# Reordering TensorE's round in a one-core image tower: second norm's turn, base products, gated turn, and who joins the turned fold

## The reference

```
h = patches(x) @ W                                  # 64 x 196 tokens, 768 -> 256
n = layernorm(h)                                    # first norm
x_proj = n @ in_w + in_b
mod    = gelu(n @ mod_w1 + mod_b1) @ mod_w2 + mod_b2        # 256 -> 1024 -> 256
y      = irfft(rfft(x_proj * mod) * rfft(kernel))   # over the 196 tokens of an image
h = h + y @ out_w + out_b
n = layernorm(h)                                    # second norm
base   = n @ base_W.T + base_b
shared = (n @ shared_A.T) @ shared_B.T
w      = softmax(n @ router_W.T + router_b), the two largest of six kept and scaled to sum 1
h = h + base + shared + sum over experts e of w_e * (n @ routed_A_e.T) @ routed_B_e.T
```

## Time and profile before

| what | value |
|---|---|
| time, median of 3 runs | 1248.58 us (1248.07 to 1249.25) |
| the profiled execution: its time, its span | 1247.64 us, 1245.8 us |
| granted TensorE clock, mean | 0.999 of full speed |
| busy: PE, PEld | 1223.9 us (98%), 1175.7 us (94%) |
| busy: DVE, ACT, POOL | 888.8 us (71%), 643.2 us (52%), 406.9 us (33%) |
| chain that ended last | PE 80%, DVE 9%, ACT 7%, issue 2%, DMA 1% |
| DMA, mean over the span | 59 GB/s |

### The profile page before, as it was taken

The page is one execution under the profiler, slowest core; times in us unless marked ns, Lnnn a source line. Parts: engine busy times, 40 slices in busy tenths (PEclk is TensorE's granted clock), DMA queues, the critical chain, the costliest instruction groups (busy, mean ns, idle before and its releaser), DMA issues.

```text
span 1245.8 us, 20849 instructions
## 1 busy us (share of the span) xinstructions
PE 1223.9 (98%) x7914; PEld 1175.7 (94%) x7914; DVE 888.8 (71%) x2591; ACT 643.2 (52%) x1197; POOL 406.9 (33%) x459
## 2 busy tenths in 40 slices
PE   9999999999999999999999999999999999999998
PEld 8899999999999999999999999999999999999996
DVE  6477766677766777766777666777667777667777
ACT  6645555545555445555455555455554445454432
POOL 3523244332244232343232443323442323433220
PEclk9999999999999999999999999999999999999999
DMA  7310222221322111222202222212221112211001
GB/s 244 94 49 20 68 69 68 56 34 47 69 69 68 56 28 55 69 68 56 59 23 68 69 68 56 33 49 68 68 69 55 26 57 68 68 56 33 14 13 34
DMA packets 85089, 72.97 MB, mean 59 GB/s; under 512 B 64775, under 2 KB 78958, under 8 KB 81150
## 3 DMA queue, kind: packets, MB, share of 16 engines
q1 hardware_dynamic: 84990, 71.66, 20.4%
HBM read 43.07 MB, written 12.85 MB: 45 GB/s over the span
## 4 chain that ended last, share of the span: by engine, by line
PE 80%; DVE 9%; ACT 7%; issue 2%; DMA 1%; SPq 1%; POOL 0%; ACTq 0%; DVEq 0%
PE rotating L1457 16%; PE rotating L1458 15%; PE rotating L1459 15%; PE rows_ps L1457 8%; PE rows_ps L1458 6%; PE rows_ps L1459 6%; PE turn L1744 5%; PE turn L1507 2%; PE rows_ps L1517 2%; ACT gelu_h L661 2%; DVE y_l L1161 1%; ACT y_h L698 1%; ACT gelu L656 1%; DVE gelu_l L1106 1%; DVE gated_l L1186 1%
## 5 line engine op out<-in xcount | busy, mean ns | idle before, releaser
L529 POOL TENSOR_TENSOR folded<-modulated 128x196 f32<-128x196 f32 x63 | 38.1, 605 | 565.0 <-DVE modulated L1118 565.0
L656 ACT ACTIVATE gelu<-rotating,consts 128x392 f32<-128x392 f32 x256 | 145.4, 582 | 109.2 <-PE rotating L1459 108.9
L514 POOL TENSOR_TENSOR gelu_l<-gelu,gelu_h 128x784 fp32r<-128x784 f32 x62 | 128.7, 2075 | 213.1 <-DVE norm L1101 172.0
L509 POOL TENSOR_TENSOR patches_l<-patches,patches_h 128x384 fp32r<-128x384 f32 (+1 forms) x186 | 182.1, 1008 | 2.8 <-ACT patches_h L608 2.8
L1457 PE MATMUL rotating<-x_h,w_h 128*128 128x392 f32 x512 | 177.2, 346 | 1.6 <-ACT gelu L656 1.6
L1457 PE MATMUL rotating<-gelu_h,w_h 128*128 128x392 f32 x512 | 177.4, 346 | 0.0
L1458 PE MATMUL rotating<-x_l,w_h 128*128 128x392 f32 x512 | 174.6, 341 | 0.0
L1459 PE MATMUL rotating<-x_h,w_l 128*128 128x392 f32 x512 | 174.6, 341 | 0.0
L1458 PE MATMUL rotating<-gelu_l,w_h 128*128 128x392 f32 x512 | 174.2, 340 | 0.0
L1459 PE MATMUL rotating<-gelu_h,w_l 128*128 128x392 f32 x512 | 174.0, 340 | 0.0
L1457 PE MATMUL rows_ps<-tokw_h,patches_h 128*128 128x256 f32 x570 | 162.9, 286 | 1.5 <-DVE patches_l L871 1.5
(11 more groups left out here) (300 smaller groups left out, 2997.7 us busy)
## 6 DMA issues: line engine op xcount, KB each, us to landing
patches<-dram_x_rest SPq DMA_DIRECT2D x30, 1152.0 KB, 5.2
out<-h_sb SPq DMA_DIRECT2D x30, 384.0 KB, 2.5
prod<-spec_y SPq DMA_TRANSPOSE x60, 3.2
patches<-dram_x_first SPq DMA_DIRECT2D x2, 384.0 KB, 5.7
h_sb<-dram_x_second SPq DMA_DIRECT2D x1, 768.0 KB, 7.6
patches<-dram_x_fourth SPq DMA_DIRECT2D x1, 768.0 KB, 9.6
h_sb<-dram_first SPq DMA_DIRECT2D x2, 320.0 KB, 3.5
gelu<-dram_w SPq DMA_DIRECT2D x1, 512.0 KB, 8.1
```

The lines of the kernel that those rows point to most:

```text
L509: pool.tensor_tensor(patches_l[:, k, 0:n], patches[:, k, 0:n], patches_h[:, k, 0:n].bitcast(F32), ALU.subtract).then_inc(pool_patches_lo, 1)
L514: pool.tensor_tensor(gelu_l[:, 2 * j:2 * j + 2, :], gelu[:, 2 * j:2 * j + 2, :], gelu_h[:, 2 * j:2 * j + 2, :].bitcast(F32), ALU.subtract)\
L529: pool.tensor_tensor(folded[:, m, 0, :, 1:NF], fwd, back, ALU.add)
L656: act.activation(gelu[:, k, :], bank(g + 1, UP[k])[:, 0:GT], ACT.Gelu, bias=b1_bias[:, k:k + 1]).then_inc(act_gelu, 1)
```

## The change

Four things move, none is computed otherwise.

1. **Second norm's turn ahead of the intake's.** `turn_x2` stood behind all of `mlp_down` 1; it now stands behind three of its eight parts, two parts ahead of `turn_x1`. Since it writes over `rows_ps`, which ScalarE's first norm reads, it also waits for `act_norm1`. ScalarE and VectorE take `x2_hi`, `x2_lo` ahead of `x1_hi`, `x1_lo`.
2. **Base products ahead of the projection.** `base_route(tail)` and with it VectorE's gate come before `project(mid)`.
3. **Gated turn behind four up blocks.** `turn_gated` moves from behind `mlp_up` 5 to behind `mlp_up` 3, `routed` from behind 6 to behind 5, `dft` from behind 7 to behind `routed`, `inverse_dft` from behind `embed` 1 to behind `embed` 0. ScalarE's `gated_hi` and `fold_hi` go ahead of its fifth gelu, VectorE's products of spectra ahead of its `gelu_lo` of the third pair.
4. **VectorE joins both halves.** `sine_whole` goes away; `join_fold` is two copies on VectorE, one behind the other, ahead of `gated_lo`.

The diff, cut to its core:

```diff
-IN, UP, TURN_GATED, OUT, DOWN = (0, 1), (2, 3, 4, 5, 6, 7, 9, 10), 8, 11, (12, 13)
+IN, UP, TURN_GATED, OUT, DOWN = (0, 1), (2, 3, 4, 5, 7, 8, 9, 10), 6, 11, (12, 13)
-TURN_AT = 5
+TURN_X2_AT, TURN_X1_AT = 3, 5
...
             def fold_hi(g):
-                    act.wait_ge(act_whole, g + 1)
-                    act.wait_ge(dve_whole, g + 1)
+                    act.wait_ge(dve_whole, 2 * g + 2)
...
                 gelu_tile(mid, 0)
-                if in_range(back):
-                    sine_whole(back)
                 gelu_tile(mid, 1)
+                gelu_hi(mid, 0)
                 gelu_tile(mid, 2)
-                gelu_hi(mid, 0)
                 gelu_tile(mid, 3)
-                gelu_tile(mid, 4)
                 if in_range(tail):
                     gated_hi(tail, bank(i, TURN_GATED))
                 if in_range(back):
                     fold_hi(back)
+                gelu_tile(mid, 4)
+                gelu_hi(mid, 1)
                 gelu_tile(mid, 5)
-                gelu_hi(mid, 1)
...
-            def cosine_whole(g):
+            def join_fold(g):
                 dve.wait_ge(fold_turned, 32 * (g + 1))
-                dve.tensor_copy(whole_halves[0:NF, 0], turned_halves[0:NF, :, 0, :]).then_inc(dve_whole, 1)
+                for x in range(2):
+                    dve.tensor_copy(whole_halves[0:NF, x], turned_halves[0:NF, :, x, :]).then_inc(dve_whole, 1)
...
                 else:
+                    if in_range(tail):
+                        base_route(tail, rows_ps, x2_h, x2_l)
                     project(mid)
-                if in_range(tail):
-                    base_route(tail, rows_ps, x2_h, x2_l)
...
                 mlp_up(mid, 3)
                 pe.wait_ge(act_gelu, HC * mid + 2)
+                if in_range(tail):
+                    turn_gated(tail, bank(i, TURN_GATED))
+                pe.wait_ge(act_gelu, HC * mid + 3)
                 mlp_up(mid, 4)
-                pe.wait_ge(act_gelu, HC * mid + 3)
+                pe.wait_ge(act_gelu, HC * mid + 4)
                 mlp_up(mid, 5)
-                pe.wait_ge(act_gelu, HC * mid + 4)
-                if in_range(tail):
-                    turn_gated(tail, bank(i, TURN_GATED))
-                pe.wait_ge(act_gelu, HC * mid + 5)
-                mlp_up(mid, 6)
                 if in_range(tail):
                     routed(tail, rows_ps)
-                pe.wait_ge(act_gelu, HC * mid + 6)
-                mlp_up(mid, 7)
                 if in_range(back):
                     dft(back)
+                mlp_up(mid, 6)
+                pe.wait_ge(act_gelu, HC * mid + 5)
+                mlp_up(mid, 7)
...
                 embed(i + 1, 0)
-                embed(i + 1, 1)
                 if in_range(back):
                     inverse_dft(back)
+                embed(i + 1, 1)
...
+                if in_range(back):
+                    mlp_down(mid, 1, range(TURN_X2_AT))
+                    pe.wait_ge(act_norm1, i + 2)
+                    turn_x2(back, rows_ps, norm2)
+                    mlp_down(mid, 1, range(TURN_X2_AT, turn_at))
...
                 turn_x1(i + 1)
                 mlp_down(mid, 1, range(turn_at, HC))
-                if in_range(back):
-                    turn_x2(back, rows_ps, norm2)
 
             last = GROUPS - 1
+            base_route(last - 2, rows_ps, x2_h, x2_l)
             project(last)
             turn_fold(last - 1)
-            base_route(last - 2, rows_ps, x2_h, x2_l)
```

More of the change, by code:

```diff
@@ L836, in _ @@
             gelu_tile(last, 3)
+            gated_hi(last - 2, bank(GROUPS, TURN_GATED))
             gelu_tile(last, 4)
@@ L1359, in _ @@
                 if in_range(back):
-                    cosine_whole(back)
+                    join_fold(back)
                 if in_range(tail):
@@ L1366, in _ @@
                     finish(tail, rows_ps)
-                for j in range(0 if i == 1 else 2, 3):
-                    gelu_lo(mid, j)
                 if in_range(back):
@@ L1372, in _ @@
                     spectrum_of_y(back)
+                for j in range(0 if i == 1 else 2, 3):
+                    gelu_lo(mid, j)
                 gelu_lo(mid, 3)
@@ L1392, in _ @@
                 modulate(mid, 0)
+                if in_range(back):
+                    x2_lo(back, rows_ps, x2_h, x2_l)
                 if i == 1:
@@ L1792, in _ @@
                 else:
+                    if in_range(tail):
+                        base_route(tail, rows_ps, x2_h, x2_l)
                     project(mid)
-                if in_range(back):
-                    if back == 0:
-                        pe.wait_ge(weight_lo, len(LATER))
-                if in_range(tail):
-                    base_route(tail, rows_ps, x2_h, x2_l)
                 if in_range(mid - 1):
@@ L1811, in _ @@
                 mlp_up(mid, 4)
[L1812 removed]
+                pe.wait_ge(act_gelu, HC * mid + 4)
                 mlp_up(mid, 5)
[L1814 to L1818 removed]
                 if in_range(tail):
                     routed(tail, rows_ps)
[L1821 to L1822 removed]
+                if back == 0:
+                    pe.wait_ge(weight_lo, len(LATER))
                 if in_range(back):
                     dft(back)
+                mlp_up(mid, 6)
+                pe.wait_ge(act_gelu, HC * mid + 5)
+                mlp_up(mid, 7)
                 if in_range(tail):
@@ L1840, in _ @@
                     embed(i + 1, 2)
+                pe.wait_ge(act_gelu, HC * mid + 6)
                 if in_range(back):
@@ L1846, in _ @@
                 pe.wait_ge(act_gelu, HC * mid + 8)
-                turn_at = 2 if i == 1 else TURN_AT
-                mlp_down(mid, 1, range(turn_at))
-                if i >= 2:
+                turn_at = 2 if i == 1 else TURN_X1_AT
+                if in_range(back):
+                    mlp_down(mid, 1, range(TURN_X2_AT))
+                    pe.wait_ge(act_norm1, i + 2)
+                    turn_x2(back, rows_ps, norm2)
+                    mlp_down(mid, 1, range(TURN_X2_AT, turn_at))
                     pe.wait_ge(dve_y, DH * back + DH)
                     pe.wait_ge(dve_h, i - 1)
+                else:
+                    mlp_down(mid, 1, range(turn_at))
                 turn_x1(i + 1)
                 mlp_down(mid, 1, range(turn_at, HC))
-                if in_range(back):
-                    turn_x2(back, rows_ps, norm2)
             last = GROUPS - 1
+            base_route(last - 2, rows_ps, x2_h, x2_l)
             project(last)
             turn_fold(last - 1)
-            base_route(last - 2, rows_ps, x2_h, x2_l)
             pe.wait_ge(dve_mod, DH * last)
@@ L1870, in _ @@
             pe.wait_ge(act_gelu, HC * last + 2)
+            turn_gated(last - 2, bank(GROUPS, TURN_GATED))
+            pe.wait_ge(act_gelu, HC * last + 3)
             mlp_up(last, 4)
-            pe.wait_ge(act_gelu, HC * last + 3)
+            pe.wait_ge(act_gelu, HC * last + 4)
             mlp_up(last, 5)
-            pe.wait_ge(act_gelu, HC * last + 4)
-            turn_gated(last - 2, bank(GROUPS, TURN_GATED))
+            routed(last - 2, rows_ps)
+            mlp_up(last, 6)
             pe.wait_ge(act_gelu, HC * last + 5)
-            mlp_up(last, 6)
-            pe.wait_ge(act_gelu, HC * last + 6)
-            routed(last - 2, rows_ps)
             mlp_up(last, 7)
```

9 lines of the change are left out of this document (1 added, 8 removed).

## The result

The changed kernel takes 1343.63 us (median of 4 runs, 1342.46 to 1344.88); the kernel before, on the same chip, 1248.32 (1247.79 to 1249.25). The ratio is 1.0763, 95% interval 1.0744 to 1.0781: 7.6% slower. The forecast of 1235.5 has the wrong sign, and the time lies above its range. The profiled execution took 1343.86 us, its span is 1340.7.

A forecast was written before the change was run, and what follows sets the result against it. TensorE's list of products was the bound, so only its standing time could be won: -31.9 + 7 + 3 + 5 + 2.6 + 1.3 = -13.0 from 1247.64, 1234.6, as a median 1235.5 us; range 1220 to 1268.

The forecast's parts named there:

- The 5.80: Time from the gate's start to the joining copy on VectorE, putting that copy at 8.97 us after the first base product.
- the stall before `routed`: TensorE's wait for the low part of the gated rows; claimed to go wholly, -12.2 us.
- +7: Port term: fold_l held until GpSimd's gelu_l ends, so dft stalls 0.24 us a round.
- The second step: On VectorE: the two joining copies run back to back, with GpSimd's gelu_l ending after them, at 12.1.
- rival 1: GpSimd gets in between VectorE's two copies; dft stalls 1.44 us a round, 1266.5 us in all; chance 0.29.
- The forecast's own mechanism: VectorE's copies back to back, GpSimd's gelu_l next, fold_l held until it ends; 1235.5 us, chance 0.49.
- The gains of the removed stalls: TensorE's waits before the mixer's output (12.2), routed (12.2) and inverse_dft (7.5) all go: -31.9 us.
- rival 2: No new stall in the rounds: port free for fold_l, landings as shown, turn waits for nothing; 1220.5 us, chance 0.15.
- Second norm's turn: On TensorE: it now waits for the first norm's scaling, losing some 0.1 us a round, +3 us.
- Late landings: The fold's transposing DMA lands late in three rounds, GpSimd goes before the first copy and dft stalls 1.6 each: +5 us.
- Ends and first fold round: Stalls in the last group (+2.6 us) and before dft in the first round with a fold (+1.3).

The follow-up runs named there:

- e1: Changed kernel with GpSimd's four later patch subtractions cut to 8 of 384 columns from round 4 on, leaving out part of the work: 1271.46 us.
- e2: Changed kernel, but GpSimd starts its first gelu_l only when both of VectorE's joining copies are done: 1302.58 us.
- e6: Changed kernel with its fourth part undone: VectorE copies the cosine half, ScalarE the sine half again: 1276.24 us.
- e3: Changed kernel with the edits of e1 and e2 together, leaving out the same work as e1: 1240.43 us.
- e4: Changed kernel with all its work, GpSimd's list reordered so no long GpSimd instruction lies beside the gate, the copies or fold_l: 1220.29 us.
- e8: Changed kernel with each of GpSimd's four later patch subtractions split into two of 192 columns, from round 4 on: 1344.61 us.
- e7: Changed kernel with gated turn, routed and dft put back behind six, seven and eight up blocks; inverse_dft left one embed behind dft: 1372.32 us.

## Why the prediction was wrong

**Two steps failed, and either alone turns the sign.** The larger is "the gate begins 3.17 after the base products do and the joining copy 5.80 after that, at 8.97". The start was right, to 0.01. The 5.80 is the gate's length at its old place, carried over to a new place without asking what runs beside it there: it came out 2.1 us longer, and e1 shows why. A wait ahead of the gated turn of 56 us stood nowhere in the sum. The prediction read GpSimd only where its `gelu_l` ran. With this step alone put right the kernel takes 1271.5 (e1).

The second is "If VectorE's two copies run back to back": they do not, GpSimd gets in between, and the second copy lasts 2.4 us in place of 0.75. That is what makes the stall before `routed`, forecast to lose 12.2 us, gain 15.5 (11.1 to 26.6), and `dft`'s of 23.7 in place of +7: both waits stay in e1, where the gate is short, and `routed`'s is gone in e2 and e6, where the gate is long. With this step alone put right the kernel takes 1302.6 (e2), with both 1240.4 (e3).

**The second step is rival 1, which came true.** It said that GpSimd gets in between the copies, and gave the times within a round nearly to the digit: the second copy ends 3.03 after the first's start (3.04 measured), `fold_l` 5.4 after it (5.39). The case against it, that VectorE may hold on, was wrong. e1, where it acts alone, took 1271.5 against the 1266.5 written down for it.

**The forecast's own mechanism** is e3: copies back to back, GpSimd next, `fold_l` held. It took 1240.4 against 1235.5; "+7 us" for the port was mis-sized, since 0.58 a round and the slow product make 19.1. Of the 0.34 that is missing a round, 0.31 is when GpSimd is done: I had it 1.7 us after the copies' end, and there it is 2.0 (619.37 to 621.38).

**The gains of the removed stalls** were right in size: y's and the spectra's went whole, and with GpSimd out of the way `routed`'s too. e4 took 1220.3; rival 2, the sum with no new stall, said 1220.5. That was not the kernel it was written for: the changed kernel reaches that state only with GpSimd's order changed.

**The smaller terms.** Second norm's turn: 1.3 us against +3. Late landings: none seen to matter against +5. In the changed kernel the copies waited for the DMA for 5.3 us in the whole run, but there the gate is late; in e1, where it is on time, they waited 5.9, and only 0.5 of it between 200 and 1190 us. Ends and first fold round: a wait of 4.3 us ahead of `dft` at the two ends, against 1.6 of standing there before, where +3.9 was forecast for all.

**How the parts add up.** Rival 1's 1266.5, the gate's 56 and some 12 us for the half clock make 1335, against 1343.6. The half clock was in no case of the prediction. What makes it fall is open: it fell ten times with 1.86, 0.78 and 0.74 us of stall a round (the changed kernel), fifteen times in e8 with much the same stalls (the first of them behind the first fold), twenty times with 1.59 and 1.94 (e7), once with 0.63 and 0.74 (e1, and once more there behind the 2.7 us wait of the first fold), and never with 1.86 and 0.74 (e2) or 1.86 alone (e6). The sum of the stalls does not order these runs.

## What to carry to other kernels

A duration read from a trace holds at its place only. Before an instruction is moved, lay every other engine's timeline beside its new place, GpSimd's first, and ask which pairs there exclude each other; one row of GpSimd (615.29 to 619.23) would have changed the forecast's sign. When VectorE's critical chain and GpSimd's bulk work exclude each other as here, give the chain a window in which GpSimd waits: here that turned a change of +7.6% into one of -2.2%, with all work kept. Moved work can come late itself: put in the kernel before, the same order made `embed` wait.

## What the runs showed of the hardware

- Beside a GpSimd subtraction a small VectorE instruction with two SBUF operands, or a TENSOR_SCALAR, on 18 columns lasts as long as GpSimd's takes to end (0.94 us beside 0.98, 0.52 beside 0.56), in place of 0.18. A TENSOR_TENSOR with an operand in PSUM and a TENSOR_REDUCE beside the same subtractions kept 0.17. The Trainium skill (SBUF — State Buffer, section "Who interferes with whom") says of such a pair that the second one "fully blocks"; the trace agrees, for instructions this small too.
- With work queued on both engines they took turns, one instruction each: GpSimd's `gelu_l` went in between VectorE's two copies (the second lasted 2.4 in place of 0.75), and each of the gate's stretched instructions went in between two of GpSimd's subtractions. e8 shows it for two sizes.
- Halving GpSimd's subtraction from 384 to 192 columns took its time only from 0.98 to 0.56 us, and did not shorten the gate.
- The granted clock went down to 1.2 GHz for 3.4 us at a time, right behind a round's stalls, in ten of the changed kernel's thirty rounds, which added some 12 of the 95 us. It did so with no single stall above 1.9 us.
